# Second layer and output of a two-layer attention and expert kernel: partitions renumbered from (position, row) to (row, position)

## The reference, cut to what matters

```python
x = x + attn_a(layernorm(x))   # heads of 8, within blocks of 64 positions of one row
x = x + ffn(layernorm(x))      # 8 experts of 512, the best 2 of each token
x = x + attn_b(layernorm(x))   # for one position, over the 16 rows, with a toroidal bias
x = x + ffn(layernorm(x))
```

## Time and profile before

| | us |
|---|---|
| median of 3 runs | 857.09 |
| lowest and highest | 852.26, 857.19 |
| the profiled execution's own time | 857.56 |
| its span | 855.4 |

### The profile page before, as it was taken

The page is one execution under the profiler, slowest core; times in us unless marked ns, Lnnn a source line. Parts: engine busy times, 40 slices in busy tenths (PEclk is TensorE's granted clock), DMA queues, the critical chain, the costliest instruction groups (busy, mean ns, idle before and its releaser), DMA issues. The chain is left out here.

```text
span 855.4 us, 27108 instructions
## 1 busy us (share of the span) xinstructions
PE 720.4 (84%) x8844; PEld 584.1 (68%) x8845; DVE 507.3 (59%) x1795; ACT 521.8 (61%) x1016; POOL 364.4 (43%) x446
## 2 busy tenths in 40 slices
PE   8888999713999999999777899976199999999950
PEld 4556667612888888888435687865078888888840
DVE  5888869751555555655265666764255565555525
ACT  4999979402666666666158888651066666666620
POOL 4356866873233333333331025677613333333320
PEclk9999989856999999999988999995599999999985
DMA  7144111121111111111252001111211111111127
GB/s 213 46 117 119 42 46 59 49 85 45 45 47 47 47 47 48 47 50 39 76 171 68 4 11 37 38 45 49 72 42 47 50 44 50 47 47 47 48 72 244
DMA packets 56731, 54.46 MB, mean 64 GB/s; under 512 B 8304, under 2 KB 47216, under 8 KB 56656
## 3 DMA queue, kind: packets, MB, share of 16 engines
q1 hardware_dynamic: 43488, 31.17, 13.1%
q0 software_dynamic: 8640, 18.11, 6.5%
q10 hardware_dynamic: 4528, 4.13, 1.5%
HBM read 29.51 MB, written 23.86 MB: 62 GB/s over the span
## 5 line engine op out<-in xcount | busy, mean ns | idle before, releaser
L1734 POOL DMA_INDIRECT expert_out<-moe_a_out,moe_a_place x71 | 68.2, 960 | 144.7 <-DVE moe_a_out L1890 144.7
L1734 POOL DMA_INDIRECT expert_out<-moe_b_out,moe_b_place x71 | 68.2, 960 | 143.9 <-DVE moe_b_out L1890 143.9
L1766 PE MATMUL wide<-wgu,moe_a_hi 128*128 x284 | 94.7, 414 | 0.0
L1766 PE MATMUL wide<-wgu,moe_b_hi 128*128 x284 | 94.3, 413 | 0.0
L1147 POOL DMA_INDIRECT routed<-stream,lb_place x64 | 62.5, 977 | 41.0 <-issue 15.7
L1782 PE MATMUL wide<-wd,moe_a_hidT 128*128 x568 | 75.3, 276 | 1.3 <-DVE moe_a_out L1890 0.7
L1782 PE MATMUL wide<-wd,moe_b_hidT 128*128 x568 | 75.3, 276 | 1.3 <-DVE moe_b_out L1890 0.7
L403 POOL DMA_INDIRECT routed<-stream,la_place x64 | 63.0, 985 | 25.2 <-issue 17.2
L1782 PEld LDWEIGHTS wide<-wd,moe_a_hidT 128*128 128x128 f32 x568 | 69.0, 192 | 2.0 <-issue 2.0
L1782 PEld LDWEIGHTS wide<-wd,moe_b_hidT 128*128 128x128 f32 x568 | 69.0, 192 | 2.0 <-issue 2.0
L1841 ACT ACTIVATE moe_a_glow<-wide 128x512 f32<-128x512 f32 x71 | 42.6, 600 | 44.0 <-PE wide L1766 44.0
(11 more groups left out here) (285 smaller groups left out, 1764.7 us busy)
## 6 DMA issues: line engine op xcount, KB each, us to landing
moe_a_rows<-routed SPq DMA_DIRECT2D x71, 67.0 KB
moe_b_rows<-routed SPq DMA_DIRECT2D x71, 67.0 KB
lb_outs<-expert_out SPq DMA_DIRECT2D x8, 512.0 KB
stream<-in_x SPq DMA_DIRECT2D x8, 256.0 KB, 6.7
la_stage<-in_wg SPq DMA_DIRECT2D x8, 256.0 KB, 2.6
la_stage<-in_wu SPq DMA_DIRECT2D x8, 256.0 KB, 3.6
wd<-in_wd SPq DMA_DIRECT2D x8, 256.0 KB, 4.6
kept<-stream SPq DMA_DIRECT2D x8, 256.0 KB, 2.5
```

Of the source, the lines that this page charges most:

```text
L1734: pool.indirect_dma_start(d.expert[:, :], bass.IndirectOffsetOnAxis(ap=place[s % 4][:, 0:1], axis=0), out[u][:, :], None).then_inc(stored[ ...
L1766: last = nc.tensor.matmul(ps[u][:, :], x[u][:, :], w(j, part), start=i == 0, stop=i == 2)
```

## The change

`crossed` now gives partition 8 s + b instead of 16 b + s, for all three of its uses, so that the outermost dim of the DRAM pattern has 16 entries instead of 8. `out_xT` writes the columns of each tile back in the order (b, s), in which the scores are taken, and `out_back` turns them to (s, b) again for the output.

```diff
 def crossed(ap, n, tiles):
 
-    return ap.rearrange("(s b m t) c -> m b s (t c)", s=ROWS, b=8, t=tiles)[bass.ds(n, 1)].rearrange("m b s x -> (m b) s x")
+    return ap.rearrange("(s b m t) c -> m s b (t c)", s=ROWS, b=8, t=tiles)[bass.ds(n, 1)].rearrange("m s b x -> (m s) b x")
...
-                nc.scalar.activation(xT[c % 2][:, :], psP[0], ACT.Copy).then_inc(copied, 1)
+                nc.scalar.activation(xT[c % 2][:, :].rearrange("p (t b s) -> p t s b", b=8, s=ROWS),
+                                     psP[0].rearrange("p (t s b) -> p t s b", b=8, s=ROWS), ACT.Copy).then_inc(copied, 1)
...
-                nc.scalar.activation(mixT[:, :], psP[0], ACT.Copy).then_inc(back_copied, 1)
+                nc.scalar.activation(mixT[:, :].rearrange("p (t s b) -> p t b s", b=8, s=ROWS),
+                                     psP[0].rearrange("p (t b s) -> p t b s", b=8, s=ROWS), ACT.Copy).then_inc(back_copied, 1)
```

## The result

The changed kernel takes 848.91 us (median of 17 runs, 845.23 to 855.56) against 853.44 us for the kernel before (17 runs, 848.88 to 863.33): a ratio of 0.9933 with a 95% interval of 0.9908 to 0.9957, a gain of 0.7% or 5.7 us (3.7 to 7.9). A second measurement of the same kernel, among the experiments, gave 0.9907 [0.9874, 0.9939]. It is less than the 1% that the prediction set as the bound of "faster" and lies inside its range. The ratios and their intervals leave out slow runs (beside copies_tile and best 6 of the 23 runs of the kernel before); the medians take all runs.

A forecast was written before the change was run, and what follows sets the result against it. TensorE is busy nearly everywhere; the opening of the second layer and the end wait for crossed DMAs on 8 of 16 engines. 2.5 + 0.9 + 3.7 = 7.1 us took 857.09 to 850.0 us, range 847 to 853.

The forecast's parts named there:

- Engines: Crossed DMAs of second layer and output: 8 outermost uses 8 of 16 engines; 16 outermost would use all.
- Rival E: Crossed DMAs: the change does not spread them, the split follows something else; 857 us, chance 0.03.
- The first load: Second layer's opening: first quad's data lands before VectorE ends its MEMSETs, so the first join gains 2.5 us.
- Rival A: Crossed loads are bound by HBM, not engines; opening gains 0, tail 3.7 us: 853.4 us, chance 0.14.
- What follows it: Opening, after the first join: TensorE idles less, so the clock gives back 0.9 us at the first projection.
- The later joins: Opening: VectorE up to 6.3 us earlier, but ACT's chain moves only 3.4 us, so the opening gives 3.4.
- D: Opening: VectorE's lead is used, giving 6.3 us instead of 3.4; 847.1 us, chance 0.10.
- The two copies: Second layer's two ACT copies with permuted writes: 0 extra taken, upper end 0.22 us a copy, 3.4 over 16.
- rival B: Each scattered element costs a second element time: 0.46 us a copy, 7.4 us for 16; 857 us, chance 0.09.
- C: Permuted copies at three element times, 0.92 us more each; 864.7 us, slower from 0.44 us a copy; chance 0.04.
- How much of it counts: Second layer's steady part, repeating every 15.7 us, is full, so extra ACT time counts as time on the path.
- The tail: End of kernel: output stores on 16 engines at 349 GB/s, latency sets the end, 853.5 to 849.8: gain 3.7 us.

The follow-up runs named there:

- copies_tile: Kernel before, old DMA patterns, with the permuted ACT copies, columns put out of order by transposes through ready-made permuted identities: ratio 1.0064 to the kernel before.
- best: perm_tile with VectorE's eight MEMSETs of ones moved behind the first join and its statistics: 846.9 us, ratio 0.9906 to the kernel before.
- ld8: Changed kernel with the 16 rows of its crossed loads written as 8 x 2, same bytes and order: ratio 0.9950 to the kernel before.
- perm_tile: Changed kernel with plain ACT copies, the transposes reading permuted identities made once as tiles: 845.8 us, ratio 0.9874 to the kernel before.
- after_again: The changed kernel itself, unaltered, measured again on the same chip: 849.83 us, ratio 0.9907 to the kernel before.
- perm_ident: Changed kernel with plain ACT copies, the transposes reading the identity with its columns permuted in place: ratio 0.9959 to the kernel before.

## Why the prediction was right or wrong

Forecast 850.0 us, a gain of 7.1; measured 848.9 against 853.4, a ratio of 0.9933, so 5.7 us (3.7 to 7.9), and 0.9907 in the repeat. Direction and size came out, and it is within 1% as forecast; but the size is in part luck, as terms were off in opposite directions.

- *Engines.* That 8 of 16 were used and that all would be: right, with both the shares and the rates doubled. The reason I gave, that 16 now stands outermost as written, is not what the runs support: written as 8 x 2 or as halves of 8 it made no difference, and that the dims collapse is the reading that fits. Rival E falls.
- *The first load.* Right: 5.97 us after the first issue against a forecast of 5.95, bound by VectorE. Rival A is ruled out here: 365 GB/s in 420 to 423 us. The Trainium skill ("DMA: Bandwidth & Descriptors", section "Latency and other measured facts") gives its 207 GB/s for rows 512 KiB apart from partition to partition. Here it is 16 and 32 KB, so no run tests it.
- *What follows it.* The clock came as forecast, 1.12 us for the projection instead of 2.01, but not by the reason alone: TensorE idled 1.84 us before the transposes and not 0.75, and in ld8 the projection took 1.88 us. What I had left out is GpSimd's root. I took the join's gain over to the norm in full, and 1.15 us of it was lost there, as the second join now runs beside it.
- *The later joins.* Right that their waits vanish from the path and that ACT's chain, not VectorE, sets the first exponential: its gain is 2.3 us and the first maximum's 4.7. D did not come.
- *The two copies.* This step failed. I took 0 "by the row that has the single-element step". They cost 0.44 and 0.50 us, almost exactly the 0.46 of rival B, twice the 0.22 that I held for the upper end. The row I leaned on is another engine's, with 64 elements and nothing to read; why it shows nothing stays open, as 64 x 0.9 ns would be half of its 112. The rule of the Trainium skill that I had cited ("Advanced Engine Details and Errata", section "SBUF Cachelines") spoke against these two copies, and it was right. B had the price of a copy right but not its total, and by C's bound of 0.44 us a copy the kernel should have become slower: both count all 16 copies in full. One of them, 0.44 us, is in the opening's 2.3 us.
- *How much of it counts.* I had counted any extra ACT time as path, from one stretch of 15.7 us, and called it a period. It is not one: `lb_xT` starts at 466.06, 481.48, 495.96, 512.15 and 528.72 us, so the quads take 14.5 to 16.6 us. By copies_tile about 3 to 5.5 of the 7.5 us count in the kernel before.
- *The tail.* Right in kind, too small in size: 5.15 us instead of 3.7. The faster stores (406 GB/s and not 349) matter little, as the sum lets latency set the new end. The mis-sized term is the old landing. I put it 0.35 us behind the last bytes, at 853.5, which leaves 1.9 us to the end of the span that would have stayed in the new tail too. It rests on 1.4 us from the issue to the first byte, which the opening's first load shows (issued at 416.95, no byte before 418.30) but not the last store of the new kernel: issued at 848.06, it moves its first bytes about 0.8 us later (DMA share 0.06 in 848.50 to 848.75, 0.40 in the next quarter). The new span ends 1.25 us after its bytes (849.75) and 2.94 us after its last issue, where the sum had 4.4.

As measured, the opening's 2.3 us (with one copy's 0.44 in it) and the tail's 5.15 make 7.4 us, and the ratio gives 5.7 (3.7 to 7.9). The 1.7 us between them is what the other 15 copies and the spread have to answer for. It is less than copies_tile's figure for 16 copies and near the 2.8 us between perm_tile and after_again, which by themselves are not clear of the noise. So the forecast of 7.1 came near because a tail 1.45 us better than forecast made up for half of the 2.8 us that the opening (1.1) and this rest (1.7) took. How large the copies' share is in the changed kernel stays open.

## What to carry to other kernels

Where a DMA share stands near a quarter or a half (0.26, 0.51) however much is queued, look at the outermost dim of its pattern, and ask which dims step evenly: here an order in which they do opened all the engines. A permutation that has to be paid on chip belongs in a transpose through a ready-made permuted identity (277 to 304 ns, as without it), or on the PSUM side of the copy (657 ns against 597); single floats written 32 or 64 bytes apart are what to avoid. Follow a gain through every engine of the chain, the short operations of GpSimd too. Judge an unseen form by a row of the same engine and length, not by a short one of another.

## What the hardware showed that was not expected

- A permuted write costs ACT 1028 to 1136 ns for 512 floats instead of 597, the same permutation read from PSUM 657; pairs of floats are nearly free (618).
- A transpose whose 128x128 identity is read with a step of 32 or 64 bytes takes 0.39 to 0.42 us (perm_ident and copies_only) where the plain ones of the same group take 0.29 and 0.36.
- Issuing got cheaper too: SyncE's issue of a crossed load takes 0.32 to 0.43 us where it took 0.57 to 0.77, as the timelines of the opening show.
- A DMA engine moves 25 GB/s of these stores whether 4, 8 or 16 work (102, 204, 406 GB/s).
- A short GpSimd operation that runs beside a join on VectorE took 0.50 to 0.68 us, and 0.20 to 0.24 where none did (L1116, L1117 and L1124 in the openings, before and after).
